# Long attention of a decoder kernel: weighing groups in pairs every fourth tick, with a ring of 12 exponentials

## What is computed

```
q = (LN(x) @ Wq).reshape(b, 100, 16, 8)            # 16 query heads
k = (context @ Wk).reshape(b, 1444, 4, 8)  # 4 key heads, 4 query heads to each
v = (context @ Wv).reshape(b, 1444, 4, 8)
scores = einsum('bqkgd,bskd->bkgqs', qg, k) / sqrt(8)
out = einsum('bkgqs,bskd->bqkgd', softmax(scores), v)
x = x + out.reshape(b, 100, 128) @ Wo
x = x + gelu(LN(x) @ sign(w1).T * mean|w1| + b1) @ sign(w2).T * mean|w2| + b2
```

## Time and profile before

| what | us |
|---|---|
| runs, lowest / median / highest | 1068.70 / 1074.39 / 1077.85 |
| the profiled execution | 1076.63 |
| its span, first to last instruction | 1074.8 |
| granted TensorE clock, mean over the span | 0.902 of full speed |
| the long attention and its block | from about 800 to the end |

### The profile page before, as it was taken

The page is one execution under the profiler, slowest core; times in us unless marked ns, Lnnn a source line. Parts: engine busy times, 40 slices in busy tenths (PEclk is TensorE's granted clock), DMA queues, the critical chain, the costliest instruction groups (busy, mean ns, idle before and its releaser), DMA issues. The chain is left out here.

```text
span 1074.8 us, 18594 instructions
## 1 busy us (share of the span) xinstructions
PE 907.2 (84%) x6319; PEld 555.0 (52%) x6328; DVE 740.8 (69%) x2034; ACT 583.3 (54%) x1772; POOL 241.7 (22%) x357
## 2 busy tenths in 40 slices
PE   7998999999797372599679799795768999999997
PEld 4447999998464130345453386492662233333333
DVE  7658777877574798475776555514658888888853
ACT  5885777777323100343535344641443777777784
POOL 5013555554200122233030000341401111111110
PEclk8999999999999685699766999996885999999999
DMA  9610000000003600000001001650212101111000
GB/s 234 156 25 2 2 1 2 2 2 1 1 1 45 78 1 15 16 1 2 0 26 31 1 1 56 180 152 17 43 27 64 25 14 18 27 28 22 2 2 16
DMA packets 76186, 35.85 MB, mean 33 GB/s; under 512 B 35236, under 2 KB 74571, under 8 KB 76092
## 3 DMA queue, kind: packets, MB, share of 16 engines
q1 hardware_dynamic: 73724, 33.61, 13.9%
q0 software_dynamic: 896, 0.63, 0.2%
q10 hardware_dynamic: 1472, 0.41, 0.2%
HBM read 24.42 MB, written 11.05 MB: 33 GB/s over the span
## 5 line engine op out<-in xcount | busy, mean ns | idle before, releaser
L679 ACT ACTIVATE L3x_E<-L3x_pS 128x400 f32<-128x400 f32 (+1 forms) x374 | 163.9, 509 | 48.2 <-PE L3x_pS L793 46.7
L521 DVE TENSOR_REDUCE L3x_NMP<-L3x_pM 128x1 f32<-128x361 f32 x384 | 176.0, 524 | 18.5 <-PE L3x_pM L770 17.5
L793 PE MATMUL L3x_pS<-ctx_tm 64*128 64x400 bf16 (+1 forms) x374 | 102.8, 347 | 5.7 <-ACT L3x_E L679 2.6
L1911 ACT ACTIVATE L0x_E<-L0x_E,ctx_r 128x100 f32<-128x100 f32 x288 | 105.1, 369 | 0.5 <-DVE L0x_E L1791 0.5
L770 PE MATMUL L3x_pM<-ctx_tm 64*128 64x361 bf16 x384 | 97.3, 336 | 3.3 <-DVE L3x_NMP L521 2.4
L810 PE MATMUL L3x_pO<-L3x_E,CT 128*32 128x400 f32 (+1 forms) x768 | 84.8, 514 | 0.6 <-ACT L3x_E L679 0.4
L770 PEld LDWEIGHTS L3x_pM<-ctx_tm 64*128 64x128 bf16 x384 | 29.3, 100 | 79.3 <-DVE L3x_NMP L521 62.6
L1720 POOL TENSOR_TENSOR L0x_E<-L0x_E,L0x_RZ 128x1200 f32<-128x1200 f32 x24 | 52.6, 2192 | 72.4 <-DVE L0x_RZ L1816 72.4
L2037 PE MATMUL L0x_pU<-ctx_tm,L0x_E 128*100 128x129 f32 x576 | 67.8, 273 | 1.1 <-POOL L0x_E L1720 1.1
L2025 PE MATMUL L0x_pS<-L0x_QS,CT 128*128 128x100 f32 x576 | 68.4, 275 | 0.0
L2025 PEld LDWEIGHTS L0x_pS<-L0x_QS,CT 128*128 128x128 f32 x576 | 66.2, 192 | 0.4 <-ACT L0x_QS L1903 0.4
(11 more groups left out here) (727 smaller groups left out, 2134.4 us busy)
## 6 DMA issues: line engine op xcount, KB each, us to landing
ctx_tm<-in_ctx SPq DMA_DIRECT2D x8, 704.0 KB
ctx_tm<-key_terms SPq DMA_DIRECT2D x16, 270.8 KB, 4.2
key_terms<-ctx_tm SPq DMA_DIRECT2D x42, 90.2 KB
ctx_tm<-in_L_ffn_wi SPq DMA_DIRECT2D x4, 512.0 KB, 7.5
ctx_tm<-in_L_ffn_wo SPq DMA_DIRECT2D x4, 512.0 KB, 7.8
ctx_tm<-query_terms SPq DMA_DIRECT2D x16, 75.0 KB, 3.3
slots_in<-L2a_zeros SPq DMA_DIRECT2D x8, 129.0 KB
L2f_XS<-slots_in SPq DMA_DIRECT2D x4, 258.0 KB, 3.1
```

The lines of the kernel that those rows point to most:

```text
L521: nc.vector.tensor_reduce(NMP[:, p, i // NC4, a, i % NC4:i % NC4 + 1], v, AX.X, ALU.max, negate=True).then_inc(s_mr, 1)
L679: nc.scalar.activation(E[0:r, n % EB, :], score_bank(n)[0:r, 0:NG * T], ACT.Exp, scale=SCALE8).then_inc(s_e, 1)
L793: nc.tensor.matmul(score_bank(n)[0:NW[k], 0:NG * T], key_rows(KS, a)[:, b % KB, k % 4, p, 128 * (k // 4):128 * (k // 4) + NW[k]], key_rows ...
L1911: last = nc.scalar.activation(E[:, n % 3, k, :], E[:, n % 3, k, :], ACT.Exp, scale=m.ctx_r[:, n % B, k:k + 1], accum_out=Z[:, n % 2, k:k + 1])
```

## The change

`EB` goes from 8 to 12. Groups are issued in pairs: a pair at start + 5, + 9 and + 13 (so at offsets 3, 7, 12, 16, 20 and 25 of a batch in the middle). At the remainders' first tick (offset 12) both remainder products go behind the tick's two scores, so just before the pair of groups of that tick; at their second tick (offset 13) both go ahead of the scores, so just behind the pair. Everything else, the jobs and the planned banks among it, stays.

```diff
-    EB = 8
+    EB = 12
...
-                r = t - start(u) - 3
-                if 0 <= r < NKT and r % 2 == 0:
+                r = t - start(u) - 5
+                if 0 <= r < NKT and r % 4 == 0:
                     return u, r // 2
...
                 for t in range(LAST + 1):
                     at_step = unit_step(t)
+                    remainder = t % PER - REM_AT if t < PER * B else None
+                    if remainder == 1:
+                        max_scores(2 * t)
+                        max_scores(2 * t + 1)
                     for a in range(2):
-                        if t < PER * B:
+                        if t < PER * B and remainder not in (0, 1):
                             max_scores(2 * t + a)
                         if at_step is not None:
                             score(*at_step, a)
+                    if remainder == 0:
+                        max_scores(2 * t)
+                        max_scores(2 * t + 1)
...
                     at_group = group_step(t)
                     if at_group is not None:
-                        weigh(*at_group)
+                        u, g = at_group
+                        weigh(u, g)
+                        weigh(u, g + 1)
```

## The result

| | before | after |
|---|---|---|
| median of 4 runs each, us | 1072.26 | 1089.29 |
| lowest to highest, us | 1068.70 to 1077.85 | 1085.92 to 1092.24 |
| ratio after/before, 95% interval | | 1.0151, 1.0114 to 1.0187 |
| the profiled execution, us | 1076.63 | 1085.92 |
| its span, us | 1074.8 | 1084.1 |

The change makes the kernel 1.5% slower; I had forecast 16.2 us, 1.5%, or 1090.5 us on the scale of the median. (With its fourth run the median of the kernel before is 1072.26, not 1074.39.)

The account below looks back on a forecast made before the run. Bound: a loop through PE, ACT and three score banks, not PE's work alone. Loss 12.5 (batches 2 to 7) + 2.6 (batch 1) + 0.4 (batch 0) + 0.7 (end) = 16.2 us: 1092.8, or 1090.5 on the median's scale; range 1071 to 1098.

Parts of the forecast that it names:

- the loop bank, reader, bank: Scores wait for exponentials to free three PSUM banks, exponentials wait for scores; this sets 2.03 us per two ticks.
- the longer stream and the burst: Between bursts eight scores run at ACT's pace, then a 1.53 us burst: 4.33 us per four ticks against 2 x 2.03.
- GpSimd's wait: Offset 20's score waits for GpSimd's sum; a group now done under that wait moves behind it: 4.72 us, now 4.00.
- PE's savings: Per batch, 1.1 us from paired groups' fewer shape changes and 0.94 us of PE work from the remainders' new place.
- The intervals: Stretches of a 26-tick batch, each ending with a burst; six forecasts sum to 30.88 us, 2.08 us more per batch.
- Six bursts of 1.53: Each batch's six bursts hold PE 1.53 us each, from 0.36 x 3 + 0.45; possible range 1.50 to 1.62.
- Batch 1: Long attention's batch without TURN and PROJ jobs, so old intervals are shorter: 2.6 us lost, estimated 2.1 to 3.0.
- The end: Behind the last maxima: 0.3 us for the last burst, 0.4 where a burst and turned rows precede the last scores.
- My term of 0.4 for a burst at the slow clock: Batch 0's first group falls in a 1.2 GHz clock; as part of a burst it delays by 0.4 us more.
- Rival A: PE's work sets the time: a batch loses 2.1 us, seven batches 14.5, result 1060 us; chance 12%.
- Rival B: Comes out even, through earlier exponentials or jobs' waits absorbing the loss: about 0.5 us a batch, result 1078; chance 18%.
- Rival C: The clock falls too, one burst per batch at 1.2 GHz: about 1 us times 7, result 1098 us; chance 8%.

Follow-up runs that it names:

- experiment 1: Kernel before with only the remainders' new place (8 exponentials, single groups): 1078.97 against 1076.95 us, ratio 1.0028.
- experiment 3: One PSUM bank moved from maxima to scores: kernel before 1076.68 us, ratio 0.9996; changed kernel 1098.63 us, ratio 1.0216; both against 1076.95 us.
- experiment 4: Exponentials over 200 of the 400 columns, in both kernels: kernel before 1060.18 us (against 1080.02 unmodified), changed kernel 1077.32 us.
- experiment 5: Half of the exponentials' and half of the maxima's columns left out, in both kernels: kernel before 1051.83 us, changed kernel 1061.48 us.

## Why the prediction was right

- **What bounds it: the loop bank, reader, bank.** Shown: halving the exponentials takes 2.2 us from a batch with PE's work untouched; taking work off PE (experiment 1) takes nothing. The prediction had one such loop, through ACT; there are two, and the one through DVE takes over as soon as the first is loosened (experiments 3 and 4).
- **Two causes, both forecast.** The intervals 0 to 12 were to lose 0.54 to the longer stream and the burst, and lost 0.48; offsets 17 to 20 were to lose 0.72 because the pair comes out from under GpSimd's wait, and lost 0.68.
- **PE's savings.** The saved shape changes are real (experiment 5, offsets 0 to 3 and 8 to 12) and off the path at full-length readers. The Trainium skill (TensorEngine Tiling (Array Packing), Tiling Modes, Key Properties) says that a change of tiling mode drains the engine; the trace agrees that it costs, about 0.10 us each by my estimate (from a group's last pass to the next product 0.45, from pass to pass 0.34 to 0.36), but no run here has it decide the time of a batch.
- **The intervals** (forecast, measured): 0 to 3 4.75, 4.71; 4 to 7 4.10, 4.16; 8 to 12 5.62, 5.55; 13 to 16 5.25, 5.21; 17 to 20 4.72, 4.67; 21 to 25 6.44, 6.38. The sum is 30.88 against 30.67. Six bursts of 1.53 for the 1.48 measured would alone make 0.3. Inside a burst of four passes the second starts 0.36 behind the first, as inside a single group, but the third and the fourth follow after 0.336 each, nearer to the group followed by a remainder; I had taken 0.36 for all.
- **The rest of the sum.** Batches 2 to 7: 6 x 1.87 = 11.2 (12.5). Batch 1, from its first maximum product to that of batch 2: 27.89, now 30.34, 2.45 (2.6). The end, from the last batch's end (1036.82, now 1045.22): 37.98, now 38.88, 0.9 (0.7). Batch 0: 26.79, now 27.62, 0.8 (0.4). Together 15.4 (16.2).
- **Batch 0: the 0.8 is the clock's and not the change's, as far as three pairs of kernels show.** Its last six ticks grew by 1.27 (6.83 to 8.10) and the twenty before them shrank by 0.44. In the kernel before the clock rose at 833.80, inside the first group and 24.5 us behind the first maximum product; in the changed kernel at 830.76, 27.5 us behind it. So the kernel before had its last two ticks and their group at full speed, and the changed one nothing but the last 0.08 us. Kernels that differ by the bursts (and the remainders' place) and whose clock rose equally late, 27.0 to 27.8 us behind the first product, take the same time for batch 0: here with halved exponentials, single and then burst,
```profile
808.89:836.78 27.89, 25.33 (x98) 6.88 (x98) 25.47 (x62) 10.42 (x36) 6.50 (x10) 0.50 0.20 48
```
```profile
810.39:838.17 27.78, 25.48 (x96) 6.95 (x96) 25.38 (x62) 10.21 (x36) 8.57 (x13) 0.50 0.20 50
```
  and 28.57 and 28.55 with four banks, 27.71 and 27.60 with the pool. My term of 0.4 for a burst at the slow clock was mis-sized: the pairs show 0.1 less to nothing. That this balance comes so near to 16.2 is in part luck: batches 1 to 7 fell 1.4 us short of the forecast, and the early clock of one execution put back 0.8. With batch 0 at 0.1 less to nothing, as in the pairs, it is 14.5.
- **Rival A** (PE's work): it fell, by experiments 1 and 4. **Rival B** (even): it fell; the three last intervals, which it would have dropped, cost 0.35, 0.68 and 0.37 (0.39, 0.72 and 0.43 forecast). Its core, that jobs' waits absorb a loss, holds the other way round: experiment 5 shows that these waits keep a loss. **Rival C** (the clock falls): not in this kernel, where the clock is full from 831 to 1060:
```profile
831.00:1060.00 229.00, 210.72 (x1633) 78.98 (x1629) 180.99 (x446) 165.20 (x397) 30.93 (x79) 1.00 0.10 16
```
but in two of its relatives the clock did fall (below).

What stays open: whether the 1.87 divides as the table of experiment 5 suggests. That experiment changes both readers at once and shortens each to a half. With the exponentials alone halved, offsets 17 to 20 lose the same 0.67, but 13 to 16 lose 0.56 (4.74, 5.30).

## What to carry to other kernels

When an engine feeds two readers through a few banks, a burst of other work on it is free only while the readers can go on with what the banks hold. Here three banks hold 1.17 us of exponentials, and the reader's pause is the time before the group (0.27), the group and the 0.40 until the next exponential, less that 1.17: 0.3 us for a group of 0.81 (0.34 seen), 1.0 for a pair of 1.48 (1.02 seen where no wait is added). Behind the burst the stream refills at the reader's step, so what batching saves on the feeding engine counts only if that engine, and not the readers, is what the waits name; count the waits between the engines before the busy shares. And look at what hides under a wait for a third engine: a third of the loss here (0.68 of 1.87) is a pair that moved from under such a wait to behind it. Where banks are short, pooling them over all streams gave more with single groups (0.7%) than moving one from one stream to another (nothing); with bursts it gave 0.10 us a batch. Try a fixed split against a pool first.

## What the runs showed of the hardware that I had not expected

- **The granted clock can fall in the middle of a stage that is at full speed otherwise.** In the changed kernel with four score banks the batch with the fall at 985.7 took 32.00 us instead of 31.05; two more falls are at 859.4 and 1043.7. In the burst kernel with halved exponentials one batch took 30.03 (918.83 to 948.86) instead of 28.48. Windows in these falls (that at 985.7 is in the window of experiment 3), first of the kernel with four banks, then of the one with halved exponentials, and the burst of the latter:
```profile
859.40:862.80 3.40, 3.40 (x22) 0.77 (x18) 0.93 (x3) 1.31 (x4) 0.00 (x0) 0.50 0.95 144
...
1043.70:1047.10 3.40, 3.40 (x22) 0.93 (x14) 0.75 (x2) 0.31 (x2) 0.00 (x0) 0.50 0.02 5
```
```profile
940.30:943.70 3.40, 3.40 (x21) 0.77 (x13) 0.97 (x3) 0.22 (x1) 0.00 (x0) 0.50 0.00 0
```
```profile
940.14 2.79 PE L811 MATMUL L3x_pO<-L3x_E,CT 128*32 128x400 f32 x16
```
All four stand at offsets 16 to 22, beside or behind the waits for NT and for GpSimd's sum. PE had holes ahead of them: it was busy 3.29, 3.29, 3.11 and 3.20 us of the last 4.0 before the falls at 859.4, 985.7, 1043.7 and 940.3. But the changed kernel has holes as long (3.08 us busy from 849 to 853) and kept its clock. Of the seven kernels with bursts two have such falls, of the six with single groups none. What decides it I have not shown.
- **When the clock rises is worth more than some terms of a sum, and a row taken across the rise prices neither level.** It rose 24.0 to 27.8 us behind the first maximum product in the kernels whose batch 0 does the full work, and batch 0 took 26.4 to 26.8 us where it rose early (24.0, 24.5) and 27.6 to 28.6 where it rose late. The kernel before is one of the early ones. Its first group, in two windows:
```profile
832.81:833.80 0.99, 0.99 (x10) 0.20 (x8) 0.99 (x3) 0.61 (x2) 0.00 (x0) 0.50 0.00 0
833.80:834.08 0.28, 0.28 (x4) 0.00 (x1) 0.27 (x1) 0.00 (x0) 0.00 (x0) 1.00 0.00 0
```
  The group holds PE 1.27 us (832.81 to 834.08) for the 0.81 at full clock, a factor of 1.6; the burst in the changed kernel 2.81 for 1.48, a factor of 1.9. The last 0.28 us of the group ran at full clock, and nearly nothing of the burst.
- **Products of four column tiles start closer together from the third pass on:** 0.336 us a pass there, 0.36 between the first two, in single groups and in bursts alike.
